# The last step sums of a graph network's node blocks: evacuated by ScalarE, added by the turning matmul, in two PSUM banks

## The reference, cut to what matters

```python
Wh = h @ W + b                                       # h: nodes after the first block, 64 features
sim = dot(Wh[row], Wh[col]) / max(|Wh[row]| * |Wh[col]|, EPS)
base = adj_v * softplus(deg_coeff[0] * deg_v + deg_coeff[1]) * (row != col)
prop_pos = segment_sum((base * relu(sim))[:, None] * Wh[col], row)
prop_neg = segment_sum((base * -relu(-sim))[:, None] * Wh[col], row)
y = softplus(scale) * (coeff[0] * prop_pos + coeff[1] * prop_neg + coeff[2] * Wh)
out = layernorm(h + y)
```

## Time and profile before

| | |
|---|---|
| median of three runs | 4748.81 us |
| profiled execution's own time | 4738.92 us |
| its span | 4736.4 us |
| TensorE matmul busy | 3146.4 us, 66% |
| VectorE busy | 3140.1 us, 66% |
| GpSimd busy | 3231.1 us, 68% |
| ScalarE busy | 1567.6 us, 33% |
| granted TensorE clock, mean | 0.844 of full |
| `product` matmuls idle before, in the whole stage `last_rows` | 85.4 us, of which 65.2 ended by VectorE's L1345 |

### The profile page before, as it was taken

The page is one execution under the profiler, slowest core; times in us unless marked ns, Lnnn a source line. Parts: engine busy times, 40 slices in busy tenths (PEclk is TensorE's granted clock), DMA queues, the critical chain, the costliest instruction groups (busy, mean ns, idle before and its releaser), DMA issues. The chain is left out here.

```text
span 4736.4 us, 63536 instructions
## 1 busy us (share of the span) xinstructions
PE 3146.4 (66%) x16141; PEld 1881.8 (40%) x16141; DVE 3140.1 (66%) x5194; ACT 1567.6 (33%) x3248; POOL 3231.1 (68%) x3224
## 2 busy tenths in 40 slices
PE   2576777777777777776555655555476767676778
PEld 2344454554455455444343443444232222322222
DVE  4677776767777677775655555554477767676787
ACT  2422232323232232323411211221344545444434
POOL 0277777777777777775377777777676777775546
PEclk6798888988888888897877777777689989889999
DMA  1233333323233332333322222222355545455556
GB/s 53 97 92 97 91 96 91 101 88 99 91 95 94 91 98 91 98 92 88 103 66 72 78 66 71 80 68 66 112 156 143 163 128 163 134 156 140 177 163 191
DMA packets 355160, 502.05 MB, mean 106 GB/s; under 512 B 92987, under 2 KB 214844, under 8 KB 354669
## 3 DMA queue, kind: packets, MB, share of 16 engines
q1 hardware_dynamic: 251549, 394.52, 25.3%
q0 software_dynamic: 100352, 102.96, 10.7%
q10 hardware_dynamic: 2896, 0.59, 0.1%
HBM read 290.63 MB, written 207.16 MB: 105 GB/s over the span
## 5 line engine op out<-in xcount | busy, mean ns | idle before, releaser
L809 POOL DMA_INDIRECT frows<-messages,fidx x2352 | 2280.6, 970 | 847.8 <-issue 669.3
L889 PE MATMUL fps_b<-hot_key,hot_lo 128*128 128x343 f32 x3136 | 1238.6, 504 | 406.4 <-PEq L70 403.7
L948 DVE TENSOR_TENSOR strip<-strip,fps_b 128x343 f32 x1568 | 787.7, 502 | 546.1 <-DVEq L70 521.6
L824 ACT ACTIVATE turned<-fps_t 128x512 f32<-128x512 f32 (+1 forms) x754 | 431.6, 572 | 1742.7 <-ACTq L70 1738.1
L879 PE MATMUL fps_sum<-hot,frows 128*64 128x80 f32 x4704 | 551.5, 302 | 600.1 <-PEq L70 600.1
L1118 POOL DMA_INDIRECT lrows<-messages,lidx x784 | 743.3, 948 | 294.5 <-issue 222.6
L889 PEld LDWEIGHTS fps_b<-hot_key,hot_lo 128*128 128x128 f32 x3136 | 544.8, 207 | 728.3 <-issue 676.3
L879 PEld LDWEIGHTS fps_sum<-hot,frows 128*64 128x64 f32 x4704 | 522.8, 195 | 691.1 <-issue 691.1
L918 DVE TENSOR_SCALAR hot_key<-iota_f,edge 128x343 f32<-128x343 f32 x1574 | 753.2, 479 | 0.1
L1284 ACT ACTIVATE pos<-l_c,coeff 128x896 f32<-128x896 f32 x392 | 394.4, 1006 | 597.6 <-PE l_c L1179 596.8
L1179 PE MATMUL l_c<-unit_t,unit_g 64*128 64x448 f32 x1568 | 437.2, 636 | 133.5 <-DVE acc L1107 72.4
(11 more groups left out here) (183 smaller groups left out, 1880.0 us busy)
## 6 DMA issues: line engine op xcount, KB each, us to landing
adj<-turned SPq DMA_DIRECT2D x696, 256.0 KB
edge<-adj SPq DMA_DIRECT2D x294, 448.0 KB
adj_x<-adj SPq DMA_DIRECT2D x98, 448.0 KB
frows<-messages,fidx POOLq DMA_INDIRECT x2352, 2.4
messages<-msg SPq DMA_DIRECT2D x14, 1120.0 KB, 4.6
lrows<-messages,lidx POOLq DMA_INDIRECT x784
adj<-turned SPq DMA_DIRECT2D x58, 64.0 KB
wh_g<-wh_rows SPq DMA_DIRECT2D x56, 32.0 KB, 1.7
```

Source lines behind the costliest of these rows:

```text
L809: pool.indirect_dma_start(rows[:, q, k, :], None, tab_l[l].ap(), bass.IndirectOffsetOnAxis(ap=idx[:, q, k:k + 1], axis=0)).then_inc(s_got[ ...
L824: act.activation(turned[j][:, 0:(b - a) * P], ps_t[j][:, 0:(b - a) * P], ACT.Copy).then_inc(s_t_free, 1)
L889: pe.matmul(ps_b[n % KB][:, 0:NT * TWIN], hot_lo[:, s % 2, k, :], hot_key[:, n % KB, :], start=True, stop=True).then_inc(s_b, 1)
L948: dve.tensor_tensor(part, part, ps_b[n % KB][:, 0:NT * TWIN].rearrange("p (h w) -> p h w", w=TWIN), ALU.add).then_inc(v, 1)
```

## The change

From visit 42 on `kept(k)` on VectorE is no more. ScalarE copies the visit's sums from PSUM to a part of `rows` (eight places of 448 columns), in the same event, ahead of `pos(u)`. The turn of steps 0 to 5 gets a second matmul for each tile, which adds the copied sums to those that `out_t` has from earlier visits; for step 6 (blocks 12 and 13, with no earlier visit) the turn reads the copied sums alone. The visits from 42 on use two PSUM banks in turn, `ps_o` and `ps_sum`, so that a visit's first product waits for the evacuation of the visit before the last one, and not of the last. For blocks 8 and up the copy waits until the turn that read the place before is done.

```diff
+                rest_t = rows[:, :, :, :].rearrange("p q k f -> p (q k f)")
+                free_from = min(k for k, (b, lo, hi) in enumerate(visits) if lo >= alone)
...
+                def bank(k):
+                    return ps_sum if k >= free_from and (k - free_from) % 2 == 1 else ps_o
+
+                def rest_of(b):
+                    return rest_t[:, b % 8 * SB:(b % 8 + 1) * SB]
+
+                def emptied(eng, k):
+                    if k < first_visit:
+                        eng.wait_ge(s_o_free, k + 1)
+                    else:
+                        eng.wait_ge(s_rest, k - first_visit + 1)
...
-                        if u == lo and k >= 1:
-                            pe.wait_ge(s_o_free, k)
+                        if u == lo:
+                            if k == free_from + 1:
+                                pe.wait_ge(s_add, n_rows)
+                            for j in range(k - 1, -1, -1):
+                                if bank(j) is bank(k):
+                                    emptied(pe, j)
+                                    break
                         weighed(pe, u)
                         for h in range(2):
-                            last = pe.matmul(ps_o[h * F:(h + 1) * F, 0:SB], wh_g[:, 2 * p + h, :], con[u % CB][:, h, :],
+                            last = pe.matmul(bank(k)[h * F:(h + 1) * F, 0:SB], wh_g[:, 2 * p + h, :], con[u % CB][:, h, :],
                                              start=(u == lo), stop=(u == hi), skip_group_check=True)
...
-                            pe.wait_ge(s_o_free, first_visit + 2 * c + 2)
+                            emptied(pe, first_visit + 2 * c + 1)
+                            if c < NCH - 1:
+                                pe.wait_ge(s_o_free, first_visit)
...
                             for j in range(CH):
-                                last = pe.matmul(ps_h[:, j * F:(j + 1) * F], out_t[:, (c * CH + j) * P:(c * CH + j + 1) * P], eye2[:, :], start=True, stop=True)
+                                if c < NCH - 1:
+                                    pe.matmul(ps_h[:, j * F:(j + 1) * F], out_t[:, (c * CH + j) * P:(c * CH + j + 1) * P], eye2[:, :], start=True, stop=False)
+                                at = c % 4 * CH * P + j * P
+                                last = pe.matmul(ps_h[:, j * F:(j + 1) * F], rest_t[:, at:at + P], eye2[:, :], start=(c == NCH - 1), stop=True)
...
+                            for k, (b, lo, hi) in enumerate(visits):
+                                if u == hi + LAG + 1 and k >= first_visit:
+                                    act.wait_ge(s_prod, hi + 1)
+                                    if k == first_visit:
+                                        act.wait_ge(s_agg, n_rows)
+                                    if b >= 8:
+                                        act.wait_ge(s_oback, (b - 8) // 2 + 1)
+                                    act.activation(rest_of(b), bank(k)[:, 0:SB], ACT.Copy).then_inc(s_rest, 1)
                             if u < len(units):
                                 act.wait_ge(s_c, u + 1)
...
-                                if u == hi + LAG + 1:
+                                if u == hi + LAG + 1 and k < first_visit:
                                     kept(k)
...
-                    dve.wait_ge(s_o_free, len(visits))
+                    dve.wait_ge(s_o_free, first_visit)
```

More of the change, by code:

```diff
@@ L1077, in last_rows @@
                 s_hot, s_wm, s_agg, s_add, s_iota = (ls(n) for n in ("hot", "wm", "agg", "add", "iota"))
-                s_c, s_pos, s_blend, s_prod, s_o_free = (ls(n) for n in ("c", "pos", "blend", "prod", "o_free"))
+                s_c, s_pos, s_blend, s_prod, s_o_free, s_rest = (ls(n) for n in ("c", "pos", "blend", "prod", "o_free", "rest"))
                 s_con = [ls(f"con{k}") for k in range(2)]
@@ L1344, in kept @@
                             dve.wait_ge(s_o_free, again[k][-1] + 1)
-                            dve.tensor_tensor(part, part, ps_o[:, 0:SB], ALU.add).then_inc(s_o_free, 1)
+                            dve.tensor_tensor(part, part, bank(k)[:, 0:SB], ALU.add).then_inc(s_o_free, 1)
                         else:
-                            dve.tensor_copy(part, ps_o[:, 0:SB]).then_inc(s_o_free, 1)
+                            dve.tensor_copy(part, bank(k)[:, 0:SB]).then_inc(s_o_free, 1)
                     def weights(r):
```

## The result

The changed kernel takes 4732.28 us (median of 7 runs, 4727.82 to 4735.54) against 4748.22 us before (7 runs, 4742.66 to 4754.69): ratio 0.9967, 95% interval 0.9956 to 0.9979. It is faster by 15.9 us; 11.7 were forecast.

A forecast was written before the change was run, and what follows sets the result against it. TensorE was taken as the bound where nothing is evacuated, VectorE from L1400 on. Waits -11.6 and the end -0.1, all else 0, gave -11.7 us: 4748.8 to 4737.1 us, range 4729 to 4746.

The forecast's parts named there:

- Waits after first visits: TensorE's waits for evacuation after visits 42 to 52 and 54, seven places, vanish: -11.6 us.
- The cause of the wait: At unit 324 the product waits for VectorE's late evacuation; with the other bank it starts 1.64 us earlier.
- The turn: Six turns grow from 7 to 14 matmuls, 1.70 to 3.40 us, hidden beside L1400 with 1.4 us of room: cost 0.
- ScalarE's copies: Copies of 0.54 us go into ScalarE's 0.85 us of idle time before `pos`: cost 0, at most 7.5 us.
- VectorE's evacuations after second visits: TensorE's 1.17 us wait goes, but VectorE's L1400 doesn't start earlier: 0, bounds 0 to 6 x 0.1 us.
- The end: The last evacuation, on the path, takes 0.54 us on ScalarE instead of 0.61 on VectorE: -0.1 us.
- The clock: TensorE falls to half clock after idle gaps; fewer gaps might gain more, but this was left to a rival, not summed.
- rival A: The clock recovers: fewer gaps mean no half-clock stretches in the output steps, -15.0 us, 4733.8 us; chance 0.20.
- B: The turn is not hidden: L1402 waits for it, -11.7 + 10.2 = -1.5 us, 4747.3 us; chance 0.11.
- C: The loop keeps the time: VectorE or ScalarE sets the next unit, only -3.8 us, 4745.0 us; chance 0.10.
- D: Low clock spreads beyond VectorE's cover after longer turns; three slow units in each of six periods, +17.1 us, 4765.9 us; chance 0.04.

The follow-up runs named there:

- e2: Changed kernel with one PSUM bank for all visits, keeping ScalarE's copies and the longer turn: ratio 0.9967 to the unchanged kernel, stage 268.86 us.
- e3: Changed kernel with each of the six turns' 14 matmuls issued twice (28): stage 278.83 us against 267.47, one run.
- e8: Unchanged kernel plus useless matmuls in two idle places of TensorE per output step, four and two: stage 280.01 us against 282.67, one run.
- e7: Changed kernel plus four useless matmuls ahead of the cosines that wait 3.46 us for VectorE: stage 267.53 us against 267.47, one run.
- e9: Unchanged kernel plus two banks, GpSimd computing skip x coeff + x a step ahead, and useless matmuls in TensorE's two idle places per period: ratio 0.9945.
- e4: Unchanged kernel plus four useless matmuls ahead of the cosines that wait 3.8 us for VectorE, in each of six output steps: ratio 1.001.
- e5: Unchanged kernel plus two banks (VectorE still evacuates, turns of 7), with GpSimd computing skip x coeff + x a step ahead: ratio 0.9951.
- e6: Changed kernel (ScalarE's copies, turns of 14) with GpSimd computing skip x coeff + x a step ahead: ratio 0.9964 to the unchanged kernel.

## Why the prediction was right, and which term was off

- **Waits after first visits, -11.6 us: right.** Where no half clock is in the way the period fell from 28.99 to 27.35, the 1.64 us worked out for unit 324; ahead of the first L1400 it is 2.04 = 1.97 + 0.07. With the 1.24 us after visit 54 that is 2.04 + 5 x 1.64 + 1.24 = 11.5 of the 15.2 us.
- **The cause of the wait: too narrow.** The text gave the gain to the second bank ("with the other bank it waits for a visit that was emptied five units before"). e2 shows that ScalarE's early copy gives it as well.
- **The turn, 0: right.** 1.6 us of room (1.4 predicted), shown by e3. The turn took 3.27 us to the next cosines (3.40 taken).
- **ScalarE's copies, 0, at 0.54 us: right.** 0.41 us of idle time remained.
- **VectorE's evacuations after second visits, 0: right.** No period shows a gain there.
- **The end, -0.1: right.** From last product to last turn 1.61 us, before 1.70.
- **The clock, 0 in the sum: the term that was mis-sized.** It was worth 3.6 us, 3.3 of them in the five periods and 0.3 behind them (so all periods are 27.35 us, where 27.4 or 28.2 were forecast). 3.3 stood in the text as rival A (chance 0.20; 4733.8 us, against 4732.3 measured), but for the wrong reason: A had the half-clock stretches vanish with the idle time. They didn't; after still has one in each period.
- **What became of the half clock.** In after each stretch adds 1.6 us to its matmuls right behind the long idle time, and TensorE still waits 0.33 us for VectorE behind it: covered. In before two of the five added 3.0 and 2.6 us there (from 4469.62 and 4528.48) and made their periods 0.9 us longer, and one more, at 4595.62, lay where nothing covers it and cost 1.55 us. e8 and e7 show the price in before (3.25 us) and in after (none).
- **Luck.** That the stretches of after came out short and in the covered place wasn't forecast, and no run shows why; e2, which has the same waits removed, lost 1.4 us of it again. To that extent the median's nearness to rival A is luck.
- **The page on the clock.** "TensorE: Matmul & The Clock Gate" of the Trainium skill, section "Why this matters for your kernels", asks for no long idle gaps; e7, e8 and e9 agree (no half clock once the long gaps are filled), but in e4 closing only the longest one made the kernel slower, with the half clock behind gaps of 0.58 and 1.93 us.
- **Rivals B, C and D fell:** L1434 doesn't wait for the turn, the units follow TensorE, and no slow stretch adds more than in before (at most 1.6 us, against 3.0).

L1400's 2.50 us, which the turn's room rests on, is 0.68 us at the end of before (4720.15), where GpSimd is idle. Beside GpSimd's weigh of 4608.84 to 4611.69 it ends 0.49 us behind that weigh, at 4612.18. The Trainium skill's "GPSIMD Engine Reference", section "1. Specifications", says that GpSimd shares its SBUF interfaces with VectorE, with contention when an instruction of VectorE has two SBUF inputs, as L1400 has; the trace agrees. Not every such instruction pays: VectorE's weigh (L1107), which starts just ahead of GpSimd's, keeps its 1.08 us.

## What to carry to other kernels

A short evacuation can be cheap on its engine and still cost, by its place in that engine's queue: the 0.61 us here cost TensorE 1.2 to 2 us each time. First see whether another bank or an idle engine already removes the wait; doing both bought 0.5 us over the bank alone and lengthened the turn. Measure a change of 0.3% in the stage that it touches, where it was 15.2 of 282.7 us, and the stage of the changed kernel repeated to 0.01 us.

## What the runs showed of the hardware

- **The clock.** In before and after TensorE's granted clock fell to the half level, 1.2 GHz, with the first cosines behind 3.46 to 3.79 us of idle time or within 2 us of their start (cosines 1.87 us instead of 1.02). The length of a shorter gap didn't decide it: after 1.93 us it fell in e4; after 1.97 us (4448.94 in before) and 1.94 us (e7) it stayed full.
- **Its price** goes by place. A stretch that adds 1.4 to 1.6 us to the matmuls cost nothing where it started 5.5 to 6.5 us behind VectorE's reader of the turn (before, after, e3, e5, e6), and all of it, 1.5 to 1.6 us, 11.6 to 13.8 us behind it (before, e3, e5, e6). In all: 3.25 us in the five periods of before, nothing in after, 3.05 us in e5.
- **VectorE beside GpSimd.** A 128x448 instruction with two SBUF inputs (L1400) took 2.50 us beside GpSimd's weigh and 0.68 us where GpSimd was idle.
